# Feed-forward of a fused decoder layer: the second half of h's codes is written by the scalar engine

## The reference

```python
def activation_quant(x, num_bits=8):
    qn = -2 ** (num_bits - 1)
    qp = 2 ** (num_bits - 1) - 1
    xf = x.astype(jnp.float32)
    s = qp / jnp.clip(jnp.max(jnp.abs(xf), axis=-1, keepdims=True), EPS, None)
    return (jnp.clip(jnp.round(xf * s), qn, qp) / s).astype(x.dtype)
...
h = jax.nn.silu(bit_linear(x, w_gate)) * bit_linear(x, w_up)
h = rms_norm(h, ln_weight)
return bit_linear(h, w_down)
```

## Time and profile before

| | us |
|---|---|
| median of 3 executions | 786.46 |
| lowest, highest | 786.3, 791.66 |
| the profiled execution, time | 788.57 |
| the profiled execution, span of the trace | 786.8 |

### The profile page before, as it was taken

One profiled execution on the slowest core, in us unless ns is written; L12 is line 12 of the kernel. 1 busy time (PEld: TensorE's weight loads), 2 busy tenths in 40 slices (PEclk: granted clock), 3 DMA queues, 4 the chain that ended last, 5 costly groups with the idle time before them and its releaser, 6 DMA issues. The chain is left out here.

```text
span 786.8 us, 14092 instructions
## 1 busy us (share of the span) xinstructions
PE 731.5 (93%) x5113; PEld 506.2 (64%) x5130; DVE 595.6 (76%) x1103; ACT 471.6 (60%) x1024; POOL 332.3 (42%) x329
## 2 busy tenths in 40 slices
PE   5988999999999999999987969999998999999993
PEld 4865777777777777777765657888874444444441
DVE  6886766885667866766677547887888999999993
ACT  4555666766676666666665314444455777677761
POOL 2011205213242134254464344445546667787661
PEclk9998999999999999999999979999999999999998
DMA  9300013214131322314311065555431233243322
GB/s 310 119 1 27 28 33 103 69 68 141 50 99 37 108 84 78 108 55 148 139 65 55 1 227 225 177 193 199 155 114 37 53 82 94 81 108 94 81 73 61
DMA packets 55218, 78.33 MB, mean 100 GB/s; under 512 B 36335, under 2 KB 38383, under 8 KB 53424
## 3 DMA queue, kind: packets, MB, share of 16 engines
q1 hardware_dynamic: 46336, 51.99, 20.9%
q0 software_dynamic: 8528, 24.93, 9.3%
q10 hardware_dynamic: 288, 0.52, 0.2%
HBM read 56.92 MB, written 17.59 MB: 95 GB/s over the span
## 5 line engine op out<-in xcount | busy, mean ns | idle before, releaser
L556 ACT ACTIVATE probs<-s_ps,neg_max 128x512 f32<-128x512 f32 (+2 forms) x256 | 152.5, 611 | 19.4 <-DVE neg_max L725 17.6
L725 DVE TENSOR_REDUCE neg_max<-s_ps 128x2 f32<-128x1024 f32 (+2 forms) x128 | 124.6, 1015 | 36.0 <-PE s_ps L963 35.6
L983 PE MATMUL pT_ps<-ident,probs 128*128 128x128 f32 x832 | 114.7, 279 | 9.6 <-DVE probs L746 8.6
L568 ACT ACTIVATE probs<-pT_ps 128x512 f32<-128x512 f32 x96 | 57.5, 599 | 98.4 <-PE pT_ps L983 97.6
L983 PEld LDWEIGHTS pT_ps<-ident,probs 128*128 128x128 f32 x832 | 93.4, 143 | 24.8 <-DVE probs L746 11.3
L746 DVE COPY probs<-pT_ps 128x512 f32<-128x512 f32 x112 | 76.8, 686 | 36.4 <-PE pT_ps L983 36.4
L1682 POOL TENSOR_TENSOR xg_own<-h,ln_w_sb 128x512 f32<-128x512 f32 x63 | 82.7, 1323 | 33.3 <-DVE h L1771 33.2
L896 PE MATMUL side_ps<-w_hi 128*128 128x512 f32 x172 | 71.1, 413 | 0.0
L420 POOL TENSOR_TENSOR aT_hi<-norm,one_col 128x512 fp32r<-128x512 f32 x15 | 15.6, 1040 | 124.8 <-DVE norm L737 86.6
L896 PE MATMUL side_ps<-w_hi,w_lo 128*128 128x512 f32 x172 | 67.5, 392 | 0.0
L896 PE MATMUL side_ps<-w_lo,w_hi 128*128 128x512 f32 x172 | 67.0, 389 | 0.0
(11 more groups left out here) (289 smaller groups left out, 1775.7 us busy)
## 6 DMA issues: line engine op xcount, KB each, us to landing
w_piece<-w_ffn SPq DMA_DIRECT2D x24, 512.0 KB, 3.6
w_stage<-w_ffn SPq DMA_DIRECT2D x12, 1024.0 KB, 4.9
xres<-x POOLq DMA_DIRECT2D x4, 1024.0 KB, 5.6
xn<-x SPq DMA_DIRECT2D x3, 1024.0 KB
x<-xres POOLq DMA_DIRECT2D x3, 1024.0 KB, 4.8
xn<-c SPq DMA_DIRECT2D x2, 1024.0 KB, 5.9
v_next<-c SPq DMA_DIRECT2D x2, 1024.0 KB, 7.6
xn<-x SPq DMA_DIRECT2D x4, 256.0 KB, 3.6
```

The source lines that it names most:

```text
L556: nc.scalar.activation(weights[qt][:, h, at:at + width(qt)], s_ps[:, h, 0:width(qt)], ACT.Exp, bias=neg_max[:, qt % 2, h:h + 1], accum_out ...
L568: nc.scalar.activation(out, turned_p, ACT.Identity).then_inc(slot_copied[0], 1)
L725: nc.vector.tensor_reduce(neg_max[:, qt % 2, 2 * s:2 * s + 2], s_ps[:, 2 * s:2 * s + 2, 0:width(qt)], AX.X, ALU.max, negate=True).then_inc ...
L983: last = nc.tensor.transpose(pT_ps[:, k % 2, h * P:h * P + P], weights[qt][:, h, a:z], ident[:])
```

## The change

The scalar engine computes the second half of the codes for tiles 0 to 14, between its pack of the first half and its pack of the second; it waits for its own result in between. The vector engine computes the first half alone, except for tile 15, where it keeps both. A constant `plus_code` is set once by GpSimd. `h_mul` and the second half of `hw` get one more reader, so the vector engine and GpSimd wait for that reader before they write them again. Two semaphores are merged to one (`rms_step`).

```diff
--- before.py
+++ after.py
@@ -1600,6 +1600,7 @@
     h_ss, h_var, h_rms = sb("h_ss", [P, 1]), sb("h_var", [P, 1]), sb("h_rms", [P, 1])
     h_top, h_max, h_inv, h_mul = sb("h_top", [P, 1]), sb("h_max", [P, 1]), sb("h_inv", [P, 1]), sb("h_mul", [P, 1])
     y_scale = sb("y_scale", [P, LATE_DOWN + 2])
+    plus_code = sb("plus_code", [P, 1])
 
     hq_code = hq_big[:].bitcast(F16)[:, 0:2 * F:2]
 
@@ -1613,8 +1614,8 @@
     gate_summed, up_summed = sem("gate_summed"), sem("up_summed")
     gate_ready, h_ready, sq_ready = sem("f_gate_ready"), sem("h_ready"), sem("sq_ready")
     hw_ready, hw_max_ready = sem("hw_ready"), sem("hw_max_ready")
-    hw_last_ready = sem("hw_last_ready")
-    ss_ready, h_var_ready, rms_ready = sem("ss_ready"), sem("h_var_ready"), sem("rms_ready")
+    hw_last_ready, hq_ready_act = sem("hw_last_ready"), sem("hq_ready_act")
+    rms_step, rms_ready = sem("rms_step"), sem("rms_ready")
     hq_step, hq_ready = sem("hq_step"), sem("hq_ready")
     h_transposed, hqT_ready = sem("h_transposed"), sem("hqT_ready")
     hq_packed, h_turned = sem("hq_packed"), [sem("h_turned0"), sem("h_turned1")]
@@ -1674,11 +1675,13 @@
                 .then_inc(y_stored[t % len(homes)], 16)
 
         def rms_of(t):
-            pool.wait_ge(h_var_ready, t + 1)
+            pool.wait_ge(rms_step, 2 * t + 2)
             nc.gpsimd.tensor_tensor(h_rms[:], h_var[:], minus_half[:], ALU.pow).then_inc(rms_ready, 1)
 
         def weighted(t, c):
             pool.wait_ge(h_ready, t * FC + c + 1)
+            if c == 2 and inside(t - 2):
+                pool.wait_ge(hq_ready_act, t - 1)
             nc.gpsimd.tensor_tensor(hw[:, t % 2, c, :], h[:, t % 2, c, :], ln_w[:, c * CHK:c * CHK + CHK], ALU.mult)\
                 .then_inc(hw_ready, 1)
 
@@ -1686,7 +1689,8 @@
         front.wait_scattered(pool, last_expert - ROW_SEMS)
         nc.gpsimd.indirect_dma_start(x2, bass.IndirectOffsetOnAxis(sh["rows"][:, last_expert:ROUTED_TILES], 0), xg[last_expert], None,
                                      bounds_check=last_row, oob_is_err=False).then_inc(front.scattered[last_expert % ROW_SEMS], 16)
-        pool.wait_ge(lnw_loaded, 16)
+        nc.gpsimd.memset(plus_code[:], CODE).then_inc(lnw_loaded, 1)
+        pool.wait_ge(lnw_loaded, 17)
         for t in range(TILES):
             if inside(t - 1):
                 rms_of(t - 1)
@@ -1720,7 +1724,13 @@
 
         def pack(t, n):
             cols = slice(n * HALF, n * HALF + HALF)
-            act.wait_ge(hq_ready, t * HALVES + n + 1)
+            if n == 0:
+                act.wait_ge(hq_ready, t + 1)
+            else:
+                act.wait_ge(hq_step, (t + 1) * HQ_STEPS)
+                nc.scalar.activation(hq_big[:, cols], flat(hw, t % 2)[:, cols], ACT.Identity, scale=h_mul[:], bias=plus_code[:])\
+                    .then_inc(hq_ready_act, 1)
+                act.wait_ge(hq_ready_act, t + 1)
             if inside(t - 1):
                 act.wait_ge(h_turned[n], t * 16)
             nc.scalar.activation(hq[:, cols], hq_code[:, cols], ACT.Identity, bias=minus_offset[:]).then_inc(hq_packed, 1)
@@ -1789,9 +1799,9 @@
 
         def sum_squares(t):
             dve.wait_ge(sq_ready, (t + 1) * HALVES)
-            nc.vector.tensor_reduce(h_ss[:], h_sq[:, t % 2, :], AX.X, ALU.add).then_inc(ss_ready, 1)
-            dve.wait_ge(ss_ready, t + 1)
-            nc.vector.tensor_scalar(h_var[:], h_ss[:], 1.0 / F, RMS_EPS, ALU.mult, ALU.add).then_inc(h_var_ready, 1)
+            nc.vector.tensor_reduce(h_ss[:], h_sq[:, t % 2, :], AX.X, ALU.add).then_inc(rms_step, 1)
+            dve.wait_ge(rms_step, 2 * t + 1)
+            nc.vector.tensor_scalar(h_var[:], h_ss[:], 1.0 / F, RMS_EPS, ALU.mult, ALU.add).then_inc(rms_step, 1)
 
         def scale_h(t):
             i = t % 2
@@ -1806,12 +1816,14 @@
             nc.vector.tensor_scalar(y_scale[:, t % (LATE_DOWN + 2):t % (LATE_DOWN + 2) + 1], h_max[:], w_mean[:, 2:3], 1.0 / QMAX, ALU.mult, ALU.mult)\
                 .then_inc(hq_step, 1)
             dve.wait_ge(hq_step, at + 4)
+            if inside(t - 1):
+                dve.wait_ge(hq_ready_act, t)
             nc.vector.tensor_scalar(h_mul[:], h_inv[:], h_rms[:], QMAX, ALU.mult, ALU.mult).then_inc(hq_step, 1)
 
         def quantize_h(t):
             i = t % 2
             dve.wait_ge(hq_step, (t + 1) * HQ_STEPS)
-            for n in range(HALVES):
+            for n in range(HALVES if t == TILES - 1 else 1):
                 cols = slice(n * HALF, n * HALF + HALF)
                 if inside(t - 1):
                     dve.wait_ge(hq_packed, (t - 1) * HALVES + n + 1)
@@ -1868,7 +1880,7 @@
     def tensor_program(pe):
         def transpose_h(t, g):
             if g % 2 == 0:
-                pe.wait_ge(hq_ready, t * HALVES + g // 2 + 1)
+                pe.wait_ge(hq_ready, t + g // 2 + 1)
             if g >= 2:
                 pe.wait_ge(hqT_ready, g - 1)
             for k in range(DK):
```

## The result

| | us |
|---|---|
| changed kernel, median of 4 executions | 805.47 |
| its lowest, highest | 803.58, 806.02 |
| kernel before, median of the 4 beside it | 788.59 |
| ratio, 95% interval | 1.0216, 1.0185 to 1.0246 |
| profiled execution, time and span | 806.02, 804.3 |

The change makes the kernel about 2.2% slower (the interval reaches from 1.9% to 2.5%). The profiled executions differ by 806.02 - 788.57 = 17.45 us.

A forecast was written before the change was run, and what follows sets the result against it. TensorE and the vector engine were nearly full, with hidden 3 waiting for gate 3 behind both packs. 13 x 1.32 = 17.2, plus 0.7 and 0.4, made 18.3 us over 786.46: 804.8 us, range 797.5 to 810.

The forecast's parts named there:

- What bounds the kernel: Steady tile: the vector engine's queue and the scalar engine's packs and gate 3 reach hidden 3 almost together, about 677.6 and 677.68.
- the vector engine's slack: Ahead of hidden 3 in a steady tile: the vector engine is ready about 0.1 us before gate 3 releases it.
- Relief at nothing: Vector engine's removed second half of the codes, 0.741 us per tile: off the path, since hidden 3 waits for gate 3.
- The price of 1.32: Scalar engine, steady tile: the second pack starts at 677.29 instead of 675.97, delaying gate 3 and hidden 3 by 1.32 us.
- the line through two sizes: Conversion's duration from activations of 2048 elements (2.091 us) and 512 (0.802): 1.23 us for 1024.
- The wait for its own result: Second pack waits for the conversion: starts 0.09 us after its end, and the 0.08 overlap between them is lost.
- The high end of 1.87: Price per tile if GpSimd's multiplication disturbed the scalar engine's read, adding 0.55 us; the prediction said it doesn't occur.
- How often: Tiles 1 to 13 at 1.32 us give 17.2, tile 14 gives 0.7, the tail 0.4: 18.3 us.
- thirteen stretches: Steady feed-forward tiles cut at code writes, from 606.87 to 740.95; the first takes 10.74 us, the last 11.04.
- The rivals: Four: vector engine as bound, 0.05; half given back, 794.7 us, 0.08; GpSimd and vector order changes, 799.3, 0.08; TensorE's clock falls, 0.01.
- The first one: Vector engine is the bound at hidden 3: 0.36 us per tile faster down to TensorE's 10.86, 4.3 us, 782; chance 0.05.
- the stretch at the lower clock: Rival of TensorE's clock falling to 1.2 GHz: tile over 20 us, more than 100 us in all; chance 0.01.

The follow-up runs named there:

- gate 3 first alone: Kernel before with gate 3 ahead of both packs, nothing moved between engines: 789.66 us, ratio 1.0004.
- the relief alone: Kernel before without the vector engine's second half of the codes in tiles 1 to 14, nothing added to the scalar engine: 786.48 us, ratio 0.9983.
- the burden alone: Kernel before plus the same conversion on the scalar engine into an unread tile, vector engine still writing both halves: 806.89 us, ratio 1.0266.
- the quarter: Changed kernel with the scalar engine converting only the last 512 columns, the vector engine the other 1536: 798.07 us, ratio 1.0147.
- the tile of 10.58 us: Steady tile of the changed kernel with conversion and gate 3 both ahead of the first pack: 784.35 us, ratio 0.9938; again 781.49, 0.9924.

## Why the prediction was right

*What bounds the kernel.* Right. Two paths of nearly equal length led to hidden 3, with gate 3 last; gate 3 first alone gave 0.12 us per tile, the 0.1 that the trace showed as the vector engine's slack.

*Relief at nothing.* Shown by the relief alone (period unchanged) and by the burden alone (the changed kernel's period to 0.01 us).

*The price of 1.32.* Measured 1.28. The duration was 1.226 us against the 1.23 of the line through two sizes; from the conversion's start to the second pack's it is 1.26, and 0.83 with the quarter, each 0.02 short of what the period grew by. The wait for its own result was over-sized: the second pack starts 0.03 after the conversion's end, not 0.09. The 0.09 came from a wait behind an accumulator read, which is another kind of instruction. Together with the lost overlap the wait is worth 0.14 per tile, where the prediction had 0.09 + 0.08.

*The high end of 1.87* didn't occur: 15 conversions lasted 1.225 to 1.229 us with the vector engine and GpSimd at work beside them. Where the conversion started together with the vector engine's half, it took 1.24 to 1.25. That isn't a sign of disturbance by itself: with the burden alone, the conversion of tile 14, which started out of an idle wait and not behind a pack, also took 1.24.

*How often.* From the first `h_mul` to the fourteenth it is 160.92 us after and 144.33 before: 16.6 for 13 tiles (17.2 predicted). Tile 14 gave 11.13 - 10.57 = 0.56 (0.71 predicted), and from the last but one `h_mul` to the end of the span it is 25.62 against 25.31, 0.31 (0.4 predicted). The sum is 17.5 against 18.3. Two readings of the prediction beside this sum were off, without weight in it. The last of its thirteen stretches is cut at the vector engine's second half (751.99); the code write is at 751.20, so that tile takes 10.25 us and not 11.04. And in tile 15 the second transposing DMA doesn't always take its 2.9 us behind the first: it landed 2.3 us after it in the changed kernel.

*Forecast and median.* The forecast of 804.8 stood against a median of 786.46 for the kernel before; the median beside the changed kernel was 788.59, and that of the changed kernel 805.47. Part of the closeness is luck: the forecast difference of 18.3 us was 1.4 more than that of the medians (16.9), and the median of the kernel before, beside the changed one, was 2.1 above the one that the forecast started from. The two errors cancel.

*The rivals.* None occurred, apart from the stretch at the lower clock in tile 1, which cost nothing there. The first one's floor was wrong, though: it took TensorE's busy time of 10.86 us per tile for its limit, and the runs reached 10.58. Had the vector engine been the bound, up to 0.64 per tile could have been gained and not 0.36. TensorE's timeline in the tile of 10.58 us shows why:

```profile
670.60 1.03 PE L1645 MATMUL e_z_ps<-w_tern,xqT_home 128*128 128x512 bf16 x4
671.46 1.03 PE L1645 MATMUL e_aT_ps<-w_tern,xqT_home 128*128 128x512 bf16 x4
...
677.50 0.39 PE L1217 MATMUL f_xT_ps<-f_ident,xq_big 128*128 128x128 f16 x4
```

A group of four matmuls counts as busy for 1.03 us, to its modelled end, but the next can start 0.86 after it. So up to 0.17 of a gap behind a group is counted as busy. Eight groups stand between 670.60 and 677.50, 6.90 us; the twelve of a tile take 10.35, and the transposes the other 0.23.

## What to carry to other kernels

Idle time of an engine has a place. An operation moved to an engine with 3 us to spare per tile cost its full duration (1.28 us for 1.23), since it stood behind the last wait and ahead of the result that the others wait for; the same operation in the gap ahead of that wait cost nothing, and with the waited-for result moved ahead as well the move was a gain. Before moving work, find the gap on the receiving engine and what ends it, and put the work into the gap, ahead of that wait; then look at what stands behind it in the order, and at the last iteration by itself.

## What the runs showed that was not expected

A scalar instruction that waits for its predecessor's result started 0.03 us after its end, and 0.13 later than one that doesn't wait (1.26 against 1.13 from start to start). A small change of order in the last tile can take back the gain of all the others: with gate 3 first the end took 3.0 us more, 1.7 of them by the lower clock, and the 15 intervals between `h_mul` steps took 1.8 less (161.93 against 163.77). TensorE's clock was granted at 0.50 for a stretch behind waits of 2.22, 3.12 and 3.59 us, and not behind others of 2.22 and 3.64, so two executions of one kernel can differ in it. In tile 1 of the changed kernel the fall cost nothing, and in the last tile, where the end hangs on these matmuls, 1.4 to 1.7 us. TensorE's busy time in a stretch with gaps (10.86 of 11.22) is not the shortest time in which it did that work (10.58).
